# Row-stacked scores of the first attention: four heads at partitions 0 to 47 and four at 64 to 111

## The chip, the cores and the metric

The kernel runs on one core of a Trainium2 chip. A core has five engines that each run their own list of instructions in order: TensorE (PE, with PEld for its weight loads), VectorE (DVE), ScalarE (ACT), GpSimd (POOL) and SyncE (SP). In this kernel SP issues every DMA. Engines meet only at semaphores. The metric is the device time of one execution in microseconds (us); smaller is better.

## The reference

The program is two transformer layers on x of shape 16 x 128 x 256 with a context of the same shape. The first attention is the part that matters here:

```python
def _L0_xattn_ref(q, k, v):                 # B = 16, D = 128 channels, T = 256
    h = 8; d = D // h                       # 8 heads of 16 channels
    qn = _l2norm(q.reshape(B, h, d, Tq), axis=-2)
    kn = _l2norm(k.reshape(B, h, d, Tk), axis=-2)
    sm = softmax(5.0 * einsum('bhdq,bhdk->bhqk', qn, kn), axis=-1)
    return einsum('bhqk,bhdk->bhdq', sm, v.reshape(B, h, dv, Tk)).reshape(B, Dv, Tq)

x = x + _L0_xattn_ref(_layernorm(x), ctx, ctx)
x = x + _L0_ffn_ref(_layernorm(x), ...)     # quantised feed-forward
x = x + _L1_xattn_ref(_layernorm(x), ctx, ...)  # second attention, 16 query heads of 128
x = x + _L1_ffn_ref(_layernorm(x), ...)     # quantised gated feed-forward
```

## The kernel before

After a barrier that ends the preparation of the weights, four stages follow: the first attention (`part_a`), a feed-forward, the second attention and another feed-forward. Each engine's program is a Python generator that is advanced in steps. The first attention has 93 steps and the first feed-forward begins at step 93 (`B_START`), so on each engine every instruction of the first attention stands ahead of every instruction of the feed-forward.

In the first attention there are 16 batches of 4 units; a unit is two heads. Every piece of work has a lag in steps behind its batch or unit (`LOAD`, `STORE`, `GATHER`, `SCORE`, ...). Inside a step the order is that of the code. One batch goes like this:

- SP loads the rows of x and of the context (L226, L227). DVE and ACT normalise them; POOL squares them (L281); PE sums the squares of each head by a matmul with a block matrix (L405) and turns the context (L401); ACT and DVE make unit vectors (L322 to L324, L375); POOL splits these into a high and a low float16 half (L287, L289).
- SP stores both halves to DRAM (L254, two DMAs), and once they have landed reads them back as stacks (`GATHER`, L242 and L245): for each head the 16 channels lie on partitions 0 to 15 with other halves of the same on 16 to 31 and 32 to 47, high, low, high for q and high, high, low for k. One matmul over 48 partitions so gives the product in nearly float32 precision. The stacks hold all eight heads side by side and are double-buffered over batches. A gather waits until its store has landed (`stored`) and until the scores of the batch two earlier are done (`scores`). SP also turns the context halves by a DMA transpose (L231).
- PE makes the scores (L391): for a unit, two heads by two halves of 128 keys, four matmuls of 256 columns. The first unit of a batch waits for the whole stack (`stacked`). The two heads of a unit write to different PSUM banks.
- ACT exponentiates a unit in one instruction (L305). PE multiplies by the values and by ones for each pair of units (L422), at four column groups of 32; DVE divides (L336, L339), POOL adds the residual (L294).

The queue of SP is in order: per batch it holds the six gather DMAs of batch b, the two stores of batch b+1, the transpose of batch b+3 and the two loads of batch b+5, and then the next gather. The transfer sizes are 64 KB for a gather DMA and 128 KB for a store or load. On PE the order per batch is: scores of units 0 and 1, values of the batch before (units 2 and 3), scores of units 2 and 3, two transposes, the sum of squares of a later batch, values of units 0 and 1.

Of the kernel before, what the change touches and what calls it, by code (L numbers as in the profile page):

```python
# [18 lines left out]
F16 = mybir.dt.float16  # L19
# [6 lines left out]
P = 128  # L26
BATCHES = 16
D = 256
# [9 lines left out]
def wait(eng, sem, value):  # L38

    if value > 0:  # L40
        eng.wait_ge(sem, value)
# [104 lines left out]
def part_a(core, x_in, ctx_in):  # L146
# [3 lines left out]
    c, nc = core, core.nc  # L150
    HEADS, HD, PAIRS = 8, 16, 4
    STACK = 3 * HD
# [15 lines left out]

    halves = c.local("halves_a", [P, 2, 2, 2 * D], F16)
    ctx_hl = c.local("ctxhl_a", [P, 2, 2, D], F16)  # L170
    q_stack = c.local("q_stack", [STACK, 2, HEADS, D], F16)
    k_stack = c.local("k_stack", [STACK, 2, HEADS, D], F16)
    yc = c.local("yc_a", [P, 4, 2, D])
    stats = c.local("stats_a", [P, 2, 6])
    mv = c.local("mv_a", [P, 2, 2])
# [13 lines left out]
    stacked = [c.sem(f"a_stacked{n}") for n in range(2)]  # L189
# [5 lines left out]
    score_banks = lambda p: c.psum[:, 2 * p:2 * p + 2, :]  # L195
# [5 lines left out]
    def heads_of(v):  # L201


        m = v % PAIRS
        return (0, 4, 1, 5)[m], (2, 6, 3, 7)[m]

    def unit(s, lag):

        v = s - lag
        return v if 0 <= v < TOTAL else None  # L210

    def batch(s, lag):

        v = s - lag
        return v // PAIRS if 0 <= v < TOTAL and v % PAIRS == 0 else None

    def sync(eng):
        for s in range(STEPS):
            b = batch(s, LOAD)
            if b is not None:  # L220
                n = b % 4

                wait(eng, S["unit"], b - 3)
                wait(eng, S["vt"], b - 3)
                wait(eng, S["ctx_low"], b - 3)
                eng.dma_start(c.x_rows[:, b, :], x_in[b, :, :]).then_inc(loaded[n], 16)  # L226
                eng.dma_start(yc[:, n, 1, :], ctx_in[b, :, :]).then_inc(loaded[n], 16)  # L227
            b = batch(s, CTX_TURN)
            if b is not None:
                eng.wait_ge(S["ctx_low"], b + 1)  # L230
                eng.dma_start_transpose(c.ctx_t[:, b, :, :].rearrange("p s (k r) -> p (s k) r", k=2),  # L231
                                        ctx_hl[:, b % 2, :, :].rearrange("p s n -> p (s n)"))\
                   .then_inc(ctx_turned[b % 2], 16)
            b = batch(s, GATHER)
            if b is not None:
                p = b % 2

                eng.wait_ge(stored[p], 32 * (b // 2 + 1))
                wait(eng, S["scores"], PAIRS * (b - 1))
                src = split_dram[p].rearrange("s (h d) n -> s d h n", d=HD)  # L240
                for k, part in enumerate((0, 1, 0)):
                    eng.dma_start(q_stack[HD * k:HD * k + HD, p, :, :], src[part, :, :, 0:D])\  # L242
                       .then_inc(stacked[p], 16)
                for k, part in enumerate((0, 0, 1)):
                    eng.dma_start(k_stack[HD * k:HD * k + HD, p, :, :], src[part, :, :, D:2 * D])\  # L245
                       .then_inc(stacked[p], 16)
            b = batch(s, STORE)
            if b is not None:
                p = b % 2

                eng.wait_ge(S["low"], b + 1)
                wait(eng, stacked[p], 96 * (b // 2))
                for part in range(2):
                    eng.dma_start(split_dram[p, part], halves[:, p, part, :]).then_inc(stored[p], 16)  # L254
            yield
        for p in range(2):
            eng.wait_ge(ctx_turned[p], 16 * (BATCHES // 2))
# [121 lines left out]
    def tensor(eng):  # L379
        eng.wait_ge(c.consts_ready, 1)  # L380
        eng.wait_ge(S["ones"], 4)
        for s in range(STEPS):
            v = unit(s, SCORE)
            if v is not None:
                b, vp = v // PAIRS, v // PAIRS % 2
                if v % PAIRS == 0:
                    eng.wait_ge(stacked[vp], 96 * (b // 2 + 1))
                wait(eng, S["exps"], v - 1)
                for j, h in enumerate(heads_of(v)):
                    for k in range(2):  # L390
                        mm = eng.matmul(score_banks(v % 2)[:, j, D * k:D * k + D], k_stack[:, vp, h, P * k:P * k + P],  # L391
                                        q_stack[:, vp, h, :], start=True, stop=True)
                mm.then_inc(S["scores"], 1)
            b = batch(s, SUM)
            if b is not None:
                n = b % 4
                eng.wait_ge(loaded[n], 32 * (b // 4 + 1))

                wait(eng, S["v_evicted"], 2 * b)
                for k in range(2):  # L400
                    t = eng.transpose(vt_half(b)[:, P * k:P * k + P], yc[:, n, 1, P * k:P * k + P], c.ident[:, :])  # L401
                t.then_inc(S["vt"], 1)
                eng.wait_ge(S["sq"], b + 1)
                wait(eng, S["clipped"], b)
                eng.matmul(LEN_BANK, c.same_head[:, :], sq[:, b % 2, :], start=True, stop=True)\  # L405
                   .then_inc(S["lengths"], 1)
            v = unit(s, VALUES)
            if v is not None and v % 2:


                b, odd = v // PAIRS, v % PAIRS // 2
                to = value_bank(b % 2)
                if not odd:
                    eng.wait_ge(S["v_evicted"], 2 * (b + 1))
                    wait(eng, S["ratio"], b - 1)
                eng.wait_ge(S["exps"], v + 1)
                for k in range(2):
                    for what in range(2):
                        for g in range(4):
                            q, j = v % PAIRS - 1 + g // 2, g % 2  # L420
                            h = 2 * g + odd
                            mm = eng.matmul(to[2 * HD * g:2 * HD * (g + 1), D * what:D * what + D],  # L422
                                            ones[:, odd, :] if what else v_t[:, b % 4, k, h, :],
                                            probs[:, q, j, k, :], start=(odd == 0 and k == 0 and what == 0),
                                            stop=(odd == 1 and k == 1 and what == 1))
                mm.then_inc(S["values"], 1)
            yield

    return sync, pool, scalar, vector, tensor


# [454 lines left out]
HEADS, KV_HEADS, HEAD_DIM = 16, 4, 128  # L886
# [581 lines left out]
def program(nc, x, ctx_in, pos_ctx, pos_x, b_w1, b_w2, wq, wk, wv, wo, q_norm, k_norm, d_w1, d_w2, d_w3,  # L1468
            inv_freq, out):
    with ExitStack() as ctx:  # L1470
# [5 lines left out]
        barrier = end_part(core, 0)  # L1476
        core.new_part()
        first = part_a(core, x, ctx_in)

        core.new_part(FFN_B_AT)  # L1480
# [74 lines left out]
```

## Time and profile before

| | |
|---|---|
| three runs, us | 799.06, 797.79, 1745.51; median 799.06 |
| the profiled execution, us | 800.01 |
| its span (first to last instruction), us | 798.3 |
| mean granted TensorE clock | 0.961 |
| busy: PE, DVE, ACT, POOL | 85%, 83%, 78%, 67% |
| first attention: first gather DMA issued, first matmul of the feed-forward, us from the span's start | 86.39, 205.94 |

Busy times say which engine did how much; the idle times say what ended each wait. SPq rows are the DMA instructions as SP's queue issues them: their duration is that of the issue, not of the transfer, whose time to landing is listed apart. The timeline merges neighbouring instructions of one line into one row with their count.

### The profile page before, as it was taken

What the parts mean: (1) busy time and instruction counts of PE and PEld (TensorE: products, weight loads), DVE (VectorE), ACT (ScalarE), POOL (GpSimd) and SP (SyncE); (2) the same over time, 40 slices, a digit from 0 to 9 for tenths busy, and PEclk for the clock granted to TensorE, in tenths of its full rate; (3) what the DMA queues carried; (4) which work ended last, traced back from release to release, by engine and by line L of the source; (5) the groups of instructions that cost most, each with busy time, mean ns of one, the idle gap of its engine ahead of it and who ended that gap; (6) DMA issues with size and microseconds to landing.
All of it is one profiled execution on the core that took longest, in us unless ns stands there. A gap on an engine that the chain in (4) does not pass through costs nothing. (4 is left out here: it accounts for less than half of the span.)

```text
span 798.3 us, 17290 instructions
## 1 busy us (share of the span) xinstructions
PE 677.3 (85%) x5139; PEld 423.0 (53%) x5139; DVE 661.1 (83%) x1576; ACT 624.3 (78%) x2122; POOL 534.5 (67%) x764
## 2 busy tenths in 40 slices
PE   0075799999578678999999999999999999978995
PEld 0043255455234345666666666666666666645552
DVE  6756556764689769999999999999999999978994
ACT  0556477777399769999999999999999999968661
POOL 1413756663357888888788878887887888753673
PEclk9997599999799989999999999999999999999997
DMA  8502555542024356897887798788879787865244
GB/s 278 199 1 54 138 155 148 142 129 86 11 67 106 64 106 126 147 144 129 148 139 142 127 154 139 134 138 154 139 135 144 143 136 133 153 113 93 58 125 122
DMA packets 323795, 99.80 MB, mean 125 GB/s; under 512 B 294868, under 2 KB 322934, under 8 KB 323446
## 3 DMA queue, kind: packets, MB, share of 16 engines
q1 hardware_dynamic: 323702, 98.70, 61.7%
q8 instruction: 41, 0.67, 0.4%
q14 instruction: 52, 0.43, 0.2%
HBM read 20.01 MB, written 6.29 MB: 33 GB/s over the span
## 5 line engine op out<-in xcount | busy, mean ns | idle before, releaser
L1235 ACT ACTIVATE psum<-psum,arena 128x256 f32<-128x256 f32 x256 | 135.9, 531 | 21.1 <-DVE arena L1355 21.0
L1311 DVE SCALAR_TENSOR_TENSOR arena<-psum,arena 128x256 f16<-128x256 f32 x256 | 110.9, 474 | 1.1 <-ACT arena L1252 1.1
L1252 ACT ACTIVATE arena<-psum,arena 128x256 f16<-128x256 f32 x256 | 100.3, 474 | 7.4 <-issue 3.4
L1444 PE MATMUL psum<-arena 128*128 128x512 f16 x384 | 94.2, 381 | 8.1 <-DVE arena L1338 7.9
L1189 POOL TENSOR_TENSOR arena<-arena 128x512 f32<-128x512 f32 x64 | 81.1, 1267 | 27.8 <-DVE arena L1330 27.8
L1406 PE MATMUL psum<-wq_t,arena 128*128 128x512 f16 x384 | 94.5, 383 | 5.5 <-ACT arena L1266 2.8
L1431 PE MATMUL psum<-arena 128*128 128x256 f16 x768 | 95.6, 275 | 1.0 <-DMA arena<-arena 0.8
L1459 PE MATMUL psum<-wo_t,arena 128*128 128x256 f16 x768 | 95.0, 274 | 0.1
L305 ACT ACTIVATE arena<-psum 128x1024 f32<-128x1024 f32 x64 | 63.1, 1019 | 33.2 <-PE psum L391 33.2
L1459 PEld LDWEIGHTS psum<-wo_t,arena 128*128 128x128 f16 x768 | 75.5, 98 | 23.2 <-issue 1.1
L1220 POOL TENSOR_TENSOR arena<-arena 128x512 f16<-128x512 f32 x64 | 74.1, 1157 | 20.0 <-DVE arena L1355 19.9
L1431 PEld LDWEIGHTS psum<-arena 128*128 128x128 f16 x768 | 75.3, 99 | 11.4 <-DMA arena<-arena 1.6
L1351 DVE TENSOR_REDUCE arena<-psum 128x4 f32<-128x1024 f32 x64 | 77.8, 1215 | 2.7 <-PE psum L1431 2.4
L1330 DVE TENSOR_TENSOR arena<-psum,arena 128x1024 f32<-128x1024 f32 x64 | 78.4, 1225 | 1.1 <-PE psum L1406 1.1
L1266 ACT ACTIVATE arena<-psum 128x128 f32<-128x128 f32 x256 | 68.2, 304 | 10.6 <-DVE arena L1330 10.6
L1417 PE MATMUL psum<-wkv_t,ctx_t 128*128 128x256 f16 x384 | 54.3, 279 | 13.2 <-DVE arena L1370 12.6
L1366 DVE SCALAR_TENSOR_TENSOR arena<-psum,arena 128x256 f32<-128x256 f32 x128 | 56.1, 480 | 9.3 <-ACT arena L1301 6.7
L1223 POOL TENSOR_TENSOR arena<-arena 128x256 f32<-128x256 f32 x64 | 46.3, 724 | 23.7 <-DVE arena L1366 23.6
L422 PE MATMUL psum<-arena 128*32 128x256 f32 x1024 | 61.9, 383 | 0.0
L1266 ACT ACTIVATION_READ_ACCUMULATOR arena<-psum 128x1 f32 x256 | 60.8, 238 | 0.0
L1444 PEld LDWEIGHTS psum<-arena 128*128 128x128 f16 x384 | 33.7, 97 | 48.0 <-issue 13.6
L1417 PEld LDWEIGHTS psum<-wkv_t,ctx_t 128*128 128x128 f16 x384 | 33.2, 99 | 46.9 <-DVE arena L1370 42.3
(187 smaller groups left out, 1612.5 us busy)
## 6 DMA issues: line engine op xcount, KB each, us to landing
arena<-split_scratch SPq DMA_DIRECT2D x96, 64.0 KB, 2.6
arena<-arena SPq DMA_TRANSPOSE x272, 3.3
split_scratch<-arena SPq DMA_DIRECT2D x32, 128.0 KB, 2.1
arena<-in_L_ffn_w SPq DMA_DIRECT2D x2, 1024.0 KB, 6.8
x_rows<-in_L_xattn_Wq SPq DMA_DIRECT2D x1, 2048.0 KB, 14.4
ctx_t<-in_L_xattn_Wo SPq DMA_DIRECT2D x1, 2048.0 KB, 12.4
x_rows<-in_x SPq DMA_DIRECT2D x16, 128.0 KB, 2.3
arena<-in_ctx SPq DMA_DIRECT2D x16, 128.0 KB, 2.5
```

Of the source, the lines that this page charges most:

```text
L1189: eng.tensor_tensor(straight(q_rot[:, :, :]), straight(q_cs[:, 0, :, :]), swapped(q_cs[:, 1, :, :]), ALU.add).then_inc(S["q_rot"], 1)
L1235: last = eng.activation(s_banks(u)[:, h, :], s_banks(u)[:, h, :], ACT.Exp, bias=bias[:, u % 2, h:h + 1], scale=r_q(u)[:, h:h + 1], accum_o ...
L1252: hi = eng.activation(p_hl[:, u % 2, 0, h, :], s_banks(u)[:, h, :], ACT.Copy, scale=share[:, u % 2, h:h + 1])
L1266: last = eng.activation(junk[:, h, :], Q_BANK[:, P * h:P * h + P], ACT.Square, accum_out=sums[:, u % 2, h:h + 1])
L1311: last = eng.scalar_tensor_tensor(p_hl[:, u % 2, 1, h, :], s_banks(u)[:, h, :], share[:, u % 2, h:h + 1], p_hl[:, u % 2, 0, h, :], ALU.mul ...
L1330: eng.tensor_tensor(q_cs[:, :, :, :], Q_BANK.rearrange("p (h d) -> p h d", h=SHARE).unsqueeze(1).broadcast_to([P, 2, SHARE, HEAD_DIM]), tu ...
L1351: eng.tensor_reduce(top[:, u % 2, :], s_banks(u), AX.X, ALU.max).then_inc(S["top"], 1)
L1406: mm = eng.matmul(Q_BANK, y_t[:, b % 2, x, k, :], c.wq_t[:, w, k, SHARE * P * g:SHARE * P * g + SHARE * P], start=(n == 0), stop=(n == 5))
L1417: mm = eng.matmul(KV_BANK[:, KEYS * row:KEYS * row + KEYS], x_t, c.wkv_t[:, w, k, g, :, :].rearrange("p a d -> p (a d)"), start=(n == 0), ...
L1431: mm = eng.matmul(s_banks(u)[:, h, :], q_head(u, q, h), k_keys(u, k), start=(n == 0), stop=(n == 2))
L1444: mm = eng.matmul(A_BANK, v[:, u % V_SLOTS, x, k, :], p_t[:, u % 2, w, :, k, :], start=(n == 0), stop=(n == 5))
L1459: mm = eng.matmul(O_BANK, a_t[:, u % 2, a, P * h:P * h + P], c.wo_t[:, w, SHARE * g + h, :], start=(g == 0 and h == 0 and n == 0), stop=(g ...
```

## The change

The stacks have 112 partitions in place of 48 and four heads side by side in place of eight: heads 0 to 3 on partitions 0 to 47, heads 4 to 7 on 64 to 111. A unit takes one head of each group, and its four matmuls alternate between the groups (and with them between the two PSUM banks). Each gather DMA is split in two, one for each group, of 32 KB in place of 64; the semaphore's targets double. In the values' loop only the index changes by which a head finds its unit's probabilities.

```diff
-    q_stack = c.local("q_stack", [STACK, 2, HEADS, D], F16)
-    k_stack = c.local("k_stack", [STACK, 2, HEADS, D], F16)
+    q_stack = c.local("q_stack", [64 + STACK, 2, HEADS // 2, D], F16)
+    k_stack = c.local("k_stack", [64 + STACK, 2, HEADS // 2, D], F16)
...
-        return (0, 4, 1, 5)[m], (2, 6, 3, 7)[m]
+        return (0, 2, 1, 3)[m], (4, 6, 5, 7)[m]
...
                 for k, part in enumerate((0, 1, 0)):
-                    eng.dma_start(q_stack[HD * k:HD * k + HD, p, :, :], src[part, :, :, 0:D])\
-                       .then_inc(stacked[p], 16)
+                    for j in range(2):
+                        eng.dma_start(q_stack[64 * j + HD * k:64 * j + HD * k + HD, p, :, :],
+                                      src[part, :, 4 * j:4 * j + 4, 0:D]).then_inc(stacked[p], 16)
                 for k, part in enumerate((0, 0, 1)):
-                    eng.dma_start(k_stack[HD * k:HD * k + HD, p, :, :], src[part, :, :, D:2 * D])\
-                       .then_inc(stacked[p], 16)
+                    for j in range(2):
+                        eng.dma_start(k_stack[64 * j + HD * k:64 * j + HD * k + HD, p, :, :],
+                                      src[part, :, 4 * j:4 * j + 4, D:2 * D]).then_inc(stacked[p], 16)
...
-                wait(eng, stacked[p], 96 * (b // 2))
+                wait(eng, stacked[p], 192 * (b // 2))
...
-                    eng.wait_ge(stacked[vp], 96 * (b // 2 + 1))
+                    eng.wait_ge(stacked[vp], 192 * (b // 2 + 1))
                 wait(eng, S["exps"], v - 1)
-                for j, h in enumerate(heads_of(v)):
-                    for k in range(2):
-                        mm = eng.matmul(score_banks(v % 2)[:, j, D * k:D * k + D], k_stack[:, vp, h, P * k:P * k + P],
-                                        q_stack[:, vp, h, :], start=True, stop=True)
+                for k in range(2):
+                    for j, h in enumerate(heads_of(v)):
+                        half = slice(64 * j, 64 * j + STACK)
+                        mm = eng.matmul(score_banks(v % 2)[:, j, D * k:D * k + D],
+                                        k_stack[half, vp, h % 4, P * k:P * k + P],
+                                        q_stack[half, vp, h % 4, :], start=True, stop=True)
...
-                            q, j = v % PAIRS - 1 + g // 2, g % 2
+                            q, j = v % PAIRS - 1 + g % 2, g // 2
```

SP's queue before, from one gather to the next; the names in brackets are the semaphores that an instruction waits for:

```order
L242 DMA arena<-split_scratch 16x8x256 [waits a_scores,a_stored0]
L242 DMA arena<-split_scratch 16x8x256 x2
L245 DMA arena<-split_scratch 16x8x256 x3
L254 DMA split_scratch<-arena 128x512 [waits a_stacked1,a_low]
L254 DMA split_scratch<-arena 128x512
L231 DMA_TRANSPOSE ctx_t<-arena 128x4x128 [waits a_ctx_low]
L226 DMA x_rows<-in_x 128x256 [waits a_ctx_low,a_vt,a_unit]
L227 DMA arena<-in_ctx 128x256
```

The same place in SP's queue of the changed kernel:

```order
L243 DMA arena<-split_scratch 16x4x256 [waits a_scores,a_stored0]
L243 DMA arena<-split_scratch 16x4x256 x5
L247 DMA arena<-split_scratch 16x4x256 x6
L256 DMA split_scratch<-arena 128x512 [waits a_stacked1,a_low]
L256 DMA split_scratch<-arena 128x512
L231 DMA_TRANSPOSE ctx_t<-arena 128x4x128 [waits a_ctx_low]
L226 DMA x_rows<-in_x 128x256 [waits a_ctx_low,a_vt,a_unit]
L227 DMA arena<-in_ctx 128x256
```

Nothing changes place; twelve DMAs of half the rows (16x4x256) stand where six (16x8x256) stood, ahead of the store of the next batch.

PE's list in the changed kernel, from the first unit of a batch to the values of its units 0 and 1 (L394 scores, L426 values, L405 transposes, L409 sum of squares):

```order
L394 MATMUL psum<-arena 128x256 [waits a_exps,a_stacked0]
L394 MATMUL psum<-arena 128x256 x3
L394 MATMUL psum<-arena 128x256 [waits a_exps]
L394 MATMUL psum<-arena 128x256 x3
L426 MATMUL psum<-arena 32x256 [waits a_exps]
L426 MATMUL psum<-arena 32x256 x15
L394 MATMUL psum<-arena 128x256 [waits a_exps]
L394 MATMUL psum<-arena 128x256 x3
L394 MATMUL psum<-arena 128x256 [waits a_exps]
L394 MATMUL psum<-arena 128x256 x3
L405 MATMUL psum<-ident,arena 128x128 [waits a_v_evicted,a_loaded2]
```

The number and order of PE's rows are those of before; only the operands' partitions and the order of the four matmuls inside a unit differ. Behind the row that waits for the stack stands all the rest of PE's work.

## Rows read from the trace of the kernel before

**Rows 1.** Timeline of PE in one batch: start us, us, what, count.
```profile
144.37 1.04 PE L391 MATMUL psum<-arena 48*128 48x256 f16 x8
145.34 1.93 PE L422 MATMUL psum<-arena 128*32 128x256 f32 x32
147.21 1.04 PE L391 MATMUL psum<-arena 48*128 48x256 f16 x8
148.19 0.44 PE L401 MATMUL psum<-ident,arena 128*128 128x128 f32 x2
148.46 1.02 PE L405 MATMUL psum<-arena,same_head 128*128 128x512 f32 x2
149.41 1.93 PE L422 MATMUL psum<-arena 128*32 128x256 f32 x32
```

**Rows 2.** Waits of PEld, 91 to 206 us: waited for, us, times, longest.
```profile
PEld psum L391 <- DMA arena<-split_scratch: 1.5, 1, 1.5
```

**Rows 3.** Timeline of SP's queue over one batch in which it never waits.
```profile
99.76 1.32 SPq L242 DMA_DIRECT2D arena<-split_scratch  x3
101.12 1.38 SPq L245 DMA_DIRECT2D arena<-split_scratch  x3
102.60 0.85 SPq L254 DMA_DIRECT2D split_scratch<-arena  x2
103.49 1.19 SPq L231 DMA_TRANSPOSE ctx_t<-arena  x1
104.79 0.52 SPq L226 DMA_DIRECT2D x_rows<-in_x  x1
105.35 0.43 SPq L227 DMA_DIRECT2D arena<-in_ctx  x1
105.90 2.48 SPq L242 DMA_DIRECT2D arena<-split_scratch  x3
```

**Rows 4.** SP's queue: first gather of the stage, one long transpose, last gather.
```profile
86.39 1.38 SPq L242 DMA_DIRECT2D arena<-split_scratch  x3
...
90.18 2.26 SPq L231 DMA_TRANSPOSE ctx_t<-arena  x1
...
191.53 2.46 SPq L242 DMA_DIRECT2D arena<-split_scratch  x3
194.03 1.38 SPq L245 DMA_DIRECT2D arena<-split_scratch  x3
```

**Rows 5.** Waits of SP's queue, 91 to 206 us.
```profile
SPq L231 <- POOL arena L273: 5.0, 7, 0.9
SPq L254 <- POOL arena L289: 3.6, 5, 1.1
SPq L41 <- PE psum L391: 1.7, 2, 0.9
SPq L242 <- DMA split_scratch<-arena: 0.9, 2, 0.5
```

**Rows 6.** Issues at the start: 8 KB in 16 rows, and 2048 KB.
```profile
0.78 0.41 SPq L937 DMA_DIRECT2D arena<-in_pos_BxS  x1
...
9.21 0.47 SPq L945 DMA_DIRECT2D x_rows<-in_L_xattn_Wq  x1
```

**Rows 7.** Source views: issue durations in ns, min/median/max.
```profile
L940 SPq DMA_DIRECT2D arena<-in_L_xattn_k_norm_w x1: 223/223/223, 2.1 to 2.1; - x1
```
**Rows 8.** The gather line, the same view.
```profile
L242 SPq DMA_DIRECT2D arena<-split_scratch x48: 318/431/1702, 86.4 to 193.6; - x48
```

**Rows 9.** DMA issues of the page: count, KB each, median us to landing.
```profile
arena<-split_scratch SPq DMA_DIRECT2D x96, 64.0 KB, 2.6
...
split_scratch<-arena SPq DMA_DIRECT2D x32, 128.0 KB, 2.1
```

**Rows 10.** PE at the end of the stage: batch 15's scores, values, first feed-forward matmul.
```profile
198.54 1.04 PE L391 MATMUL psum<-arena 48*128 48x256 f16 x8
199.51 1.93 PE L422 MATMUL psum<-arena 128*32 128x256 f32 x32
201.38 1.04 PE L391 MATMUL psum<-arena 48*128 48x256 f16 x8
202.35 3.66 PE L422 MATMUL psum<-arena 128*32 128x256 f32 x64
205.94 0.39 PE L860 MATMUL psum<-cs_b,minus_off 128*128 128x512 f16 x1
```

**Rows 11.** Stretches: us, busy of PE, PEld, DVE, ACT, POOL (counts), PEclk, DMA share, GB/s.
```profile
100.00:104.00 4.00, 4.00 (x51) 2.49 (x50) 1.12 (x3) 2.60 (x3) 1.67 (x2) 1.00 0.64 190
...
208.00:212.00 4.00, 0.00 (x0) 0.00 (x0) 2.97 (x14) 0.00 (x0) 1.92 (x6) 0.86 0.00 0
```

## The prediction, on record before the changed kernel ran

> **What bounds the kernel now.** I went from the stage table of the page (the first attention runs from about 86 to 206 us) to the timeline of PE, then to PE's waits, and then to the queue of SP, since the change touches both. In the timeline of PE a batch is a closed row of work: 144.37 to 151.28 us, a period of 6.9 us in which scores (0.97 us from their start to the next start), values (1.87), transposes (0.27) and the sum of squares (0.95) follow each other [rows 1]. For the stacks PE waited once, 1.5 us, in the whole stage [rows 2]. So PE sets the pace, and shorter scores look like a gain. The second thing to see is how close SP is behind. From 99.76 to 105.90 SP never waits, and one batch takes it 6.14 us of pure issuing [rows 3]. Over the stage, from the first gather at 86.39 to the end of the last at 195.41 [rows 4], that is 109.0 us, and its waits add up to 5.0 + 3.6 + 1.7 + 0.9 = 11.2 us [rows 5]. SP is a second engine at its limit: 97.8 of 109.0 us are issuing.
>
> **What the change does, part by part.**
>
> *PE's scores.* Eight matmuls of two units take 0.97 us, 0.12 each [rows 1]. If matmuls in different row groups overlap in pairs, half goes: 0.49 us for each pair of units, 0.97 per batch. The trace has no row-grouped matmul. The nearest row is the values: 32 passes in four column groups of a length of 1.93 us, 0.06 each, against about 0.5 for one pass of twice the columns in the sum of squares (two passes in 1.02 us) [rows 1], so groups of columns do overlap. Bounds: nothing and 0.97 us per batch. I take the whole, since the two heads also write different banks; in the forecast it counts only in the last batch, 0.9 us.
>
> The Trainium skill ("TensorE: Matmul & The Clock Gate", part 3, packing small matmuls) says that matmuls on distinct row groups run concurrently, and that 32-row tiles gained about three times. By that rule PE's period would be 5.9 us and 16 batches would give back up to 15.5 us, were PE still the bound; no run here shows it yet.
>
> *SP's queue.* Six gather DMAs become twelve. From the first gather's issue to the store behind it the six take 102.60 − 99.76 = 2.84 us, 0.473 each with the gap [rows 3]. What does one of half the size cost? The issue hardly depends on size: 8 KB in 16 rows took 0.41 us, 2048 KB took 0.47 [rows 6], a gather of 64 KB 0.43, a store or load of 128 KB 0.42 to 0.52 [rows 3, 8]. The cheapest gather took 0.318 [rows 8] and a single row of 0.5 KB 0.223 [rows 7]; these are the lower bounds (with 0.04 us of gap, 0.36 and 0.26). Half a gather still has 16 rows of partitions, so I take 0.473: twelve take 5.68 us, and SP's batch becomes 6.14 + 2.84 = 8.98 us. That is above PE's 6.9 (or 5.9), so SP becomes the bound and PE waits for the stacks.
>
> The sum along SP's queue, from the first gather at 86.39 [rows 4]:
> - Batches 0 to 10, each with store, transpose and loads of later batches behind the gathers: 11 × 8.98 = 98.8.
> - Batches 11 to 14: the loads are over and from 13 on the transposes too, and the next gather must wait for its store to land. The second store is issued 0.45 after the first and lands 2.1 later [rows 3, 9]: 4 × (5.68 + 0.45 + 2.1) = 32.9.
> - The last gather: eleven issues, then 2.6 us until the twelfth has landed [rows 9]: 5.2 + 2.6 = 7.8.
> - Stalls. One transpose took 2.26 us in place of 1.19, one gather of three 2.48 in place of 1.32 [rows 3, 4]. Their total is what is left: regular issuing is 11 × 6.14 + 2 × 5.03 + 2 × 3.73 + 2.8 = 87.9 us (without loads 5.03, without transpose too 3.73), with 11.2 of waits 99.1; 9.9 us of the 109.0 remain, on 161 issues. With 257 issues that makes 15.8 if each issue has its share, 12.6 if they come with time. I take 14.
>
> The twelfth gather DMA of batch 15 so lands at 86.4 + 98.8 + 32.9 + 7.8 + 14 = 239.9 us. Before, the scores of batch 15 started at 198.54 and the feed-forward's first matmul at 205.94 [rows 10]; of these 7.4 us the faster scores take 0.9, so the stage ends at 246.4 instead of 205.94. On each engine the feed-forward stands behind the stage, so nothing hides the 40.5 us, and nothing later gets shorter. The profiled execution took 800.0 (span 798.3), which is 0.9 above the median of 799.06: 840.5 by the profile, **839** against the median.
>
> *Waits behind the gathers.* The store, transpose and loads now stand 2.84 us later behind each gather; their consumers are whole batches away. The nearest is the load of batch b+5, which waits for unit vectors of batch b+2 made behind the values on PE; PE now stands idle about 4 us per batch, so they are ready. The wait for the scores of two batches earlier (1.7 us in all [rows 5]) ends early for the same reason. The doubled semaphore targets and the new index cost nothing. The same bytes move: 768 rows of 512 bytes for a batch, in twelve DMAs.
>
> **The rivals.**
>
> 1. *The issue follows the size* (the other side: not slower). SP stays hidden as long as twelve issues plus their stalls fit into the 11.2 us of waits, 0.7 us per batch: an issue of at most 0.26 us, or 0.22 with the stalls. For it: 0.223 for a single row [rows 7]. Against it: 16 rows at 0.41 and 2048 KB at 0.47 [rows 6]. At 0.215 the queue gains 0.22 × 16 + 96 × 0.062 = 9.5 us, less than its waits, and the stage ends 1.7 + 0.9 us earlier: **797**. Even were the six more DMAs free, SP's own 97.8 us bound the gain at 11.2 + 0.9: 788. That is why faster by over 2% has next to no chance. The Trainium skill ("DMA: Bandwidth & Descriptors", issuing engines are not separate DMA queues) calls the sequencer's time to initiate a DMA usually small relative to the DMA itself; by that rule splitting costs about nothing, and the time would be this rival's. Here the issue takes 0.43 us of 2.6 to landing, but there are eleven such DMAs in a batch of 6.9 us.
> 2. *A price in between*: 0.318 + 0.04 for each [rows 8]. Twelve take 4.3, 1.4 us less than I sum for each of 16 batches: 839 − 22 = **817**. Against it: it is the minimum of 48, and the median is 0.431.
> 3. *The clock falls.* PE's work is 5.9 us of a period of about 9.9 with stalls, so it stands idle 4.0 us at a stretch. After the last matmul of the stage (ending near 206.3) the stretch from 208 to 212 has a mean of 0.86: full speed until about 210.9, 4.6 us later, then 1.2 GHz [rows 10, 11]. That is close. At half speed PE's batch would be nearly 12 us, above SP's 9.9, so it would then run without a pause; a few batches would lose about 2 us each and the last 6 us once: **850**.
> 4. *The pairs don't overlap*: PE's batch stays 6.9, still under SP's, and only the last 0.9 us are lost: 840. It is not told from the forecast by the time.
>
> **How the numbers follow.** The forecast (with rival 4) has 0.80. Its own range goes from 830 (0.41 + 0.04 per issue: −4.5; stalls as before, 10: −4) to 848 (stalls of 16, a slower landing, some of rival 3). Rival 3 has 0.07, rival 2 0.05, rival 1 0.07, something faster still 0.01. A range of 820 to 852 leaves out rivals 1 and most of 2 and the end of 3, and some of the unknown in the stalls. Two per cent of 799 is 16 us, about what a measurement of this kernel can tell from none: slower than 815 are the forecast, rival 3 and more than half of rival 2, 0.90; within 2% 0.09; faster 0.01.
>
> **What would show it.** In the changed kernel's profile: SP's gather lines with 96 issues each at a median near 0.43 us; an interval between gathers of 9 to 10 us in place of 6.1 to 7.9, with almost no waits of SP's queue before batch 11; PE waiting for DMA about 4 us once per batch at the scores; scores of two units in about 0.6 us in place of 1.04; the first matmul of the feed-forward near 246 us; and everything after it as long as before. I am wrong if the issues come out at 0.3 us or less, or if the next gather waits for something else than the queue, such as unit vectors or the landing of the stores.

## The result and the profile after

The changed kernel takes 833.6 us (median of four runs, 831.62 to 835.03) against 798.67: a ratio of 1.044 with a 95% interval of 1.041 to 1.047, so slower by 4.4%. One of the four runs of the kernel before took 1745.51 us; it is left out of the ratio. The forecast was 839, its range 820 to 852. The profiled execution took 834.02 with a span of 832.3; before it was 800.01 and 798.3.

The timeline of SP's queue over one batch of the changed kernel; it answers to [rows 3]:

```profile
96.43 2.78 SPq L243 DMA_DIRECT2D arena<-split_scratch  x6
99.25 2.77 SPq L247 DMA_DIRECT2D arena<-split_scratch  x6
102.11 0.84 SPq L256 DMA_DIRECT2D split_scratch<-arena  x2
103.00 1.19 SPq L231 DMA_TRANSPOSE ctx_t<-arena  x1
104.30 0.51 SPq L226 DMA_DIRECT2D x_rows<-in_x  x1
104.86 0.43 SPq L227 DMA_DIRECT2D arena<-in_ctx  x1
105.39 2.72 SPq L243 DMA_DIRECT2D arena<-split_scratch  x6
```

From gather to gather it is 8.96 us (8.98 were forecast), and there is no wait in it. The source view of one gather line, in ns, min/median/max, answers to [rows 8]; the DMA issues of the page answer to [rows 9]:

```profile
L247 SPq DMA_DIRECT2D arena<-split_scratch x96: 313/426/1847, 88.9 to 233.4; - x96
```
```profile
arena<-split_scratch SPq DMA_DIRECT2D x192, 32.0 KB, 1.8
...
split_scratch<-arena SPq DMA_DIRECT2D x32, 128.0 KB, 1.8
```

Half the bytes cost the same 0.43 us to issue. What did get shorter is the landing, 1.8 us in place of 2.6. The waits of SP's queue in the stage, 86 to 245 us, answer to [rows 5]:

```profile
SPq L243 <- DMA split_scratch<-arena: 2.7, 2, 1.4
SPq L231 <- POOL arena L275: 1.9, 3, 0.8
```

11.2 us of waits before, 4.6 now, and only 1.9 of these for another engine: SP is the bound. PE's weight loads, which stand ahead of its matmuls, wait instead, where [rows 2] had one wait of 1.5 us:

```profile
PEld psum L394 <- DMA arena<-split_scratch: 45.0, 16, 4.9
```

PE in one batch and at the end of the stage, which answers to [rows 1, 10]; the brackets give the idle time of PE and what ended it:

```profile
142.80 0.61 PE L394 MATMUL psum<-arena 48*128 48x256 f16 x8 [1.54 <-DMA arena<-split_scratch]
143.34 1.93 PE L426 MATMUL psum<-arena 128*32 128x256 f32 x32
...
161.70 1.03 PE L394 MATMUL psum<-arena 48*128 48x256 f16 x8 [3.75 <-DMA arena<-split_scratch]
162.66 3.64 PE L426 MATMUL psum<-arena 128*32 128x256 f32 x32
...
235.23 0.61 PE L394 MATMUL psum<-arena 48*128 48x256 f16 x8 [2.94 <-DMA arena<-split_scratch]
235.77 3.19 PE L426 MATMUL psum<-arena 128*32 128x256 f32 x32
238.90 0.98 PE L394 MATMUL psum<-arena 48*128 48x256 f16 x8
239.81 3.66 PE L426 MATMUL psum<-arena 128*32 128x256 f32 x64
243.40 0.39 PE L864 MATMUL psum<-cs_b,minus_off 128*128 128x512 f16 x1
```

Three things are to be seen. The pairing works: eight score matmuls take 0.61 us where they took 1.04, and the next work starts 0.54 after them where it was 0.97, so 0.43 us of 0.97 are gone for two units. (The four matmuls of a unit also alternate between the PSUM banks now; no run does that without row groups, so the 0.43 us belong to the two together.) The stage ends at 243.40, 37.5 us later than before. And after some of the pauses the clock is at its lower level: scores of 1.03, values of 3.64.

```profile
140.00:160.00 20.00, 13.72 (x192) 6.48 (x184) 11.89 (x27) 12.14 (x19) 10.87 (x14) 1.00 0.39 108
160.00:180.00 20.00, 15.46 (x168) 7.01 (x168) 10.07 (x20) 10.75 (x16) 9.16 (x13) 0.83 0.40 110
```

These two stretches (the columns of [rows 11]) show how a granted clock of 0.83 raises PE's busy time from 13.7 to 15.5 us for fewer instructions. PE's busy share is no measure of work here.

### The profile page after: what moved, and what is told of

Its sections match the earlier page's. It is cut to its first block and busy times, and to the rows that moved or that the text cites. A ratio compares the mean times of both kernels' runs of the same rounds, so it can differ in the third digit from the quotient of the medians.

```text
span 832.3 us, 17386 instructions
## 1 busy us (share of the span) xinstructions
PE 679.5 (82%) x5139; PEld 415.2 (50%) x5139; DVE 662.2 (80%) x1576; ACT 625.5 (75%) x2122; POOL 534.2 (64%) x764
## 5 line engine op out<-in xcount | busy, mean ns | idle before, releaser
L426 PE MATMUL psum<-arena 128*32 128x256 f32 x1024 | 74.8, 442 | 0.0
L289 POOL CAST arena<-arena 128x512 f16<-128x512 f32 x16 | 10.8, 673 | 71.2 <-DVE arena L377 71.2
```

## The experiments

Theory A is the forecast's: SP's queue bounds the stage, and what counts is how many DMAs it issues. Its rival B puts the loss on the new layout, the alternation or the falling clock.

**split_only**: only the DMAs, without row groups.

```diff
-                    eng.dma_start(q_stack[HD * k:HD * k + HD, p, :, :], src[part, :, :, 0:D])\
-                       .then_inc(stacked[p], 16)
+                    for j in range(2):
+                        eng.dma_start(q_stack[HD * k:HD * k + HD, p, 4 * j:4 * j + 4, :],
+                                      src[part, :, 4 * j:4 * j + 4, 0:D]).then_inc(stacked[p], 16)
...
```

> The kernel before, with each gather DMA split in two by heads (12 of 32 KB for a batch) into the old stacks of 48 partitions; PE's scores stay as they were. Theory A (SP's queue is the bound, its cost is the number of issues): the stage is as long as in the changed kernel but for the faster scores of the last batch, 0.9 us: 834 to 836 us. Theory B (the slowdown comes from the new layout, the alternation on PE or the clock that falls behind it): about 799 us, as before.

Measured: 834.5 us, ratio 1.0455 (1.0426 to 1.0484). The split alone makes the whole loss, on the old layout and with the old order on PE; B falls.

**tiny_rows and tiny_one**: the kernel before with six more DMAs for a batch, of 16 rows and of one row.

```diff
+                for n in range(6):
+                    eng.dma_start(spare[0:16, p, n, :], split_dram[p, 0, 0:16, 0:8]).then_inc(stacked[p], 16)
...
```

In tiny_one `spare[0:1, ...]` and `split_dram[p, 0, 0:1, 0:8]` stand in their places.

> The kernel before with six more DMAs for a batch behind the gathers, each of 16 rows of 16 bytes (256 bytes) into a spare tile. Theory A (number of issues): as the kernel with twelve halved gathers, 832 to 838 us. Rival (issue follows rows or bytes): 799 to 806 us.

> The same with each of the six extra DMAs a single row of 16 bytes. If an issue costs the same whatever its rows: 832 to 838 us. If a single row costs the 0.22 us that the constants' loads showed: 6 x 0.26 = 1.6 us for a batch, 25 us and 6 of stalls less 11 of waits that are free: 815 to 820 us.

Measured: 833.15 us, 1.0405 (1.038 to 1.043), and 814.89, 1.0184 (1.0156 to 1.0211), just under the 815 to 820 of a cheap single row. The source view of the added line, first with 16 rows, then with one:

```profile
L249 SPq DMA_DIRECT2D arena<-split_scratch x96: 323/421/1890, 88.9 to 233.7; - x96
```
```profile
L249 SPq DMA_DIRECT2D arena<-split_scratch x96: 228/253/326, 88.8 to 216.0; - x96
```

256 bytes in 16 rows cost 0.42 us of the queue, as do 32, 64 and 128 KB; the time is that of the changed kernel. A single row costs 0.25, and the kernel loses less than half as much. So neither the bytes nor the number of transfers (six more in both runs) are the price but the issue. Of the sizes that were run only the single row issues faster; between one row and 16 nothing was tried.

**split_one**: one of the six gather DMAs split, seven for a batch.

```diff
+                    for a, z in (((0, 4), (4, 8)) if n < 1 else ((0, 8),)):
+                        eng.dma_start(stack[HD * k:HD * k + HD, p, a:z, :], src[part, :, a:z, at:at + D])\
+                           .then_inc(stacked[p], 16)
...
```

> The kernel before with one of the six gather DMAs split (seven for a batch). Theory A with SP's free 11.2 us: 16 x 0.47 = 7.6 us and 1 of stalls are less than that: 798 to 801 us. Rival (each further issue costs its share of the whole, 35 us / 6): 804 to 806 us.

Measured: 799.04 us, 0.9997 (0.9984 to 1.0011). The first further DMA is free: the loss has a threshold. SP's waits in the stage, 11.2 us before, are down to 5.2 (2.1 + 1.4 + 1.0 + 0.7 in the same view); they paid for it.

**half_act**: the changed kernel, the upper group's six gather DMAs issued by ACT, ahead of the exponential in its program.

```diff
+            b = batch(s, GATHER)
+            if b is not None:
+                p, j = b % 2, 1
+                eng.wait_ge(stored[p], 32 * (b // 2 + 1))
+                wait(eng, S["scores"], PAIRS * (b - 1))
...
```

> The changed kernel, with the six gather DMAs of the upper group issued by ACT in place of SP. Theory A: SP issues six again (6.1 us for a batch and stalls), but ACT pays 6 x 0.47 = 2.8 us on top of 5.7 us of its own work, 8.5 us for a batch, so ACT becomes the bound: 815 to 822 us. If issuing were free on ACT: 786 to 798 us. If not SP's queue but the twelve transfers themselves were the bound: 833 us.

Measured: 812.69 us in two runs, 1.0167 (1.0129 to 1.0205), 2 us below the 815 to 822 that were expected. ACT's timeline in one batch, and PE's wait for ACT from 86 to 230 us:

```profile
144.43 0.20 ACT L330 ACTIVATE arena<-arena 128x1 f32<-128x1 f32 x1
144.49 1.30 ACTq L310 DMA_DIRECT2D arena<-split_scratch  x3
145.81 3.24 ACTq L313 DMA_DIRECT2D arena<-split_scratch  x3
149.15 2.86 ACT L319 ACTIVATE arena<-psum 128x1024 f32<-128x1024 f32 x3 [4.52 <-issue]
```
```profile
PE psum L406 <- ACT arena L319: 23.3, 22, 3.5
```

ACT computes nothing while it issues, 4.5 us here, and PE then waits for the exponentials; for the stacks it waited once, 1.1 us. Another queue helps, but its engine pays about the same for a DMA (a median of 0.45 us), stalls among them.

**filler**: the changed kernel with more work on PE.

```diff
+                for again in range(2):
+                    eng.matmul(LEN_BANK, c.same_head[:, :], sq[:, b % 2, :], start=True, stop=True)
```

> The changed kernel, with the sum of squares of each batch computed three times over into the same bank (only the last signals), 1.9 us more of work on PE for a batch in the time in which it waits for the stacks. Theory A: PE's 7.9 us stay under SP's 9.2 to 9.4, the clock stays at 2.4 GHz and the time at 831 to 835 us. If the falling clock had a part in the slowdown: 820 to 828 us. If PE's work were on the path: 16 x 1.9 = 30 us more, over 860.

Measured: 838.28 us, 1.0465 (1.0438 to 1.0492): 4.7 us above the changed kernel and 3 above what was expected. The waits of SP's queue show it:

```profile
SPq L256 <- POOL arena L291: 8.7, 4, 6.9
```

The longer sum of squares comes ahead of the unit vectors, and a store now waited 6.9 us for them. It is the first store, before the stage gets going, and the first gather behind it issues at 89.53 where the changed kernel has 86.11:

```profile
89.53 2.77 SPq L243 DMA_DIRECT2D arena<-split_scratch  x6
```

That is 3.4 of the 4.7 us; the stretch behind the stage has 1.9 more (590.8 against 588.9). From the first gather to the feed-forward's first matmul (246.15) this kernel takes 156.6 us, the changed one 157.3. So 1.9 us more of work for each batch cost nothing inside the stage, where 30 would be due: PE is off the path. On the clock it is no clean test, since the edit added waits; but from 100 to 240 us the granted clock rose in six of seven stretches of 20 us, to 1.00 in five of them, and the stage became hardly shorter. The changed kernel's own waits set a limit: the first scores of all 16 batches waited for the stacks, and SP waited for another engine 1.9 us. By these rows the falling clock can't have cost more than that ahead of the last batch, where it cost 1.7.

**merged_only and merged_pairs**: the issues taken away, without and with the row groups. DRAM now holds for each channel its three stack rows (high, low, high beside high, high, low), so that 48 rows are one DMA. The gather and the store of merged_pairs, against the changed kernel:

```diff
+                src = split_dram[p].rearrange("(h d) (t a) n -> (d t) h (a n)", d=HD, a=2)
+                for j in range(2):
+                    eng.dma_start(stack[64 * j:64 * j + STACK, p, :, :], src[:, 4 * j:4 * j + 4, :]).then_inc(stacked[p], 16)
...
-                for part in range(2):
-                    eng.dma_start(split_dram[p, part], halves[:, p, part, :]).then_inc(stored[p], 16)
+                four = halves[:, p, :, :].rearrange("p s (a n) -> p (s a) n", a=2)
+                for to, at in ((slice(0, 2), slice(0, 2)), (slice(2, 4), slice(2, 0, -1)), (slice(4, 6), slice(0, 4, 3))):
+                    eng.dma_start(split_dram[p, :, to, :], four[:, at, :]).then_inc(stored[p], 16)
```

> The kernel before, with the stack laid out in DRAM by three stores of 128 KB (row order channel by channel, high, low, high beside high, high, low) and gathered by one DMA of 384 KB for a batch; PE as before. Theory A: SP needs 4.2 us for a batch, PE's 6.9 us bound the stage as before: 796 to 800 us. Theory B says the same, so this run is the base for the next one.

> The changed kernel's row groups and alternating scores, with three stores and two gather DMAs of 192 KB for a batch in place of two and twelve. Theory A: SP needs 4.7 us for a batch and no longer bounds; the scores of two units take 0.54 in place of 0.97 us, 16 x 0.86 = 13.8 us less on PE: 784 to 789 us, if ACT's 5.7 us for a batch leave PE its 6.0. Theory B: no faster than 799 us.

Measured: 798.16 us, 0.9989 (0.998 to 0.9997), and 795.0 us, 0.9945 (0.9927 to 0.9963). Relieving SP is worth next to nothing by itself, as expected. With it the row groups no longer cost, but of 13.8 us expected 4.5 came, 3.2 of them against merged_only. PE's timeline of merged_pairs, one batch and the next:

```profile
150.95 0.61 PE L388 MATMUL psum<-arena 48*128 48x256 f16 x8
151.49 1.93 PE L420 MATMUL psum<-arena 128*32 128x256 f32 x32
153.36 0.61 PE L388 MATMUL psum<-arena 48*128 48x256 f16 x8
154.19 0.41 PE L399 MATMUL psum<-ident,arena 128*128 128x128 f32 x2 [0.22 <-DVE arena L352]
156.07 1.12 PE L403 MATMUL psum<-arena,same_head 128*128 128x512 f32 x2 [1.47 <-POOL arena L277]
157.13 1.93 PE L420 MATMUL psum<-arena 128*32 128x256 f32 x32
158.99 0.61 PE L388 MATMUL psum<-arena 48*128 48x256 f16 x8
```

This batch takes 8.04 us and the one ahead of it (from 144.65) 6.3: on every second one PE waits 1.5 us for POOL's squares (L277). The kernel before has the same pattern, only hidden from my reading. Its next batch after that of [rows 1] has this row:

```profile
156.29 1.13 PE L405 MATMUL psum<-arena,same_head 128*128 128x512 f32 x2 [0.76 <-POOL arena L281]
```

Its scores start at 144.37, 151.28 and 159.21: 6.9 and 7.9 by turns, 7.4 on average. POOL's list in merged_pairs explains it:

```profile
151.28 0.73 POOL L283 CAST arena<-arena 128x512 f16<-128x512 f32 x1 [3.30 <-DVE arena L371]
152.08 1.16 POOL L285 TENSOR_TENSOR arena<-arena 128x512 f16<-128x512 f32 x1
153.21 0.72 POOL L290 TENSOR_TENSOR x_rows<-arena,x_rows 128x256 f32<-128x256 f32 x1
153.87 0.40 POOL L267 CAST arena<-arena 128x256 f16<-128x256 f32 x1
154.35 0.67 POOL L269 TENSOR_TENSOR arena<-arena 128x256 f16<-128x256 f32 x1
154.98 1.04 POOL L277 TENSOR_TENSOR arena<-arena 128x512 f32<-128x512 f32 x1
```

The squares stand behind the halves of the unit vectors (L283, L285), the residual (L290) and the context's halves (L267, L269), and all of these hang on DVE's work behind the values of the batch before. Shorter scores only lengthen PE's wait in this loop.

Two of the five waits for the squares cost more than themselves. The values behind them took 3.59 and 3.40 us in place of 1.93, and these batches 9.7:

```profile
126.77 3.59 PE L420 MATMUL psum<-arena 128*32 128x256 f32 x32
```

From 126.77 to 130.30 the granted clock was 0.52, after PE had waited 1.48 us; behind the other three such waits the values took 1.93 us. So 3.3 us of what the pairs failed to bring went to the clock.

**only_pool and pairs_pool**: POOL squares first, then adds the residual, then makes the context's halves.

```diff
-    LOAD, STATS, RSTD, ROWS, CTX_HALVES, CTX_TURN, SQUARE, SUM, CLIP, CTX, LENGTH = 0, 3, 4, 5, 5, 7, 6, 8, 9, 10, 11
+    LOAD, STATS, RSTD, ROWS, CTX_HALVES, CTX_TURN, SQUARE, SUM, CLIP, CTX, LENGTH = 0, 3, 4, 5, 5, 7, 5, 8, 9, 10, 11
...
+            b = batch(s, SQUARE)
...
+            b = batch(s - 1, RESIDUAL)
...
```

Both blocks now stand ahead of CTX_HALVES; the squares come a step earlier, and the residual a step later.

> The kernel with two gather DMAs and paired scores (795 us), whose batches took 6.3 and 8.0 us by turns: on every second one PE waited about 1.5 us for POOL's squares, which stand behind the residual and the context's halves. Here POOL squares first, then adds the residual, then makes the context's halves. Theory C (this chain over DVE and POOL held the pairs' gain back): no wait for the squares, every batch at 6.0 to 6.4 us, 16 x 1.1 = 17 us less than before: 780 to 787 us. Rival (ACT's exponentials are the next bound, or the clock falls in PE's pauses): 790 to 795 us.

> The same order on POOL in the kernel with one gather DMA and unpaired scores (798 us), whose batches took 6.9 and 7.9 us by turns. Theory C: every batch at PE's own 6.9 us, half a microsecond less on twelve batches: 791 to 794 us. Rival: 797 to 799 us.

Measured: 786.69 us, 0.9836 (0.9821 to 0.985), and 797.27, 0.9975 (0.9965 to 0.9985). PE's timeline of pairs_pool:

```profile
121.47 0.61 PE L388 MATMUL psum<-arena 48*128 48x256 f16 x8
122.01 1.93 PE L420 MATMUL psum<-arena 128*32 128x256 f32 x32
123.88 0.61 PE L388 MATMUL psum<-arena 48*128 48x256 f16 x8
124.70 0.41 PE L399 MATMUL psum<-ident,arena 128*128 128x128 f32 x2 [0.21 <-DVE arena L352]
124.95 1.02 PE L403 MATMUL psum<-arena,same_head 128*128 128x512 f32 x2
125.90 1.93 PE L420 MATMUL psum<-arena 128*32 128x256 f32 x32
```

The next batch starts at 127.77: 6.30 us, with no wait for the squares. From the second to the twelfth every batch takes 6.3 us (one 6.6), and none has values at the lower clock. Theory C holds, and this is the fastest version here, 1.6% ahead of the kernel before. Its stage ends at 195.49, against 205.94 before. only_pool misses what was expected by 3 us and lands in the rival's range, 797 to 799, although each of its batches takes 6.9 us (scores at 103.16, 110.07, 116.98), as Theory C says. The head of the stage took the gain back: with the context's halves behind the squares SP's first transpose came later, and behind it in SP's queue the first gather:

```profile
87.07 1.21 SPq L230 DMA_TRANSPOSE ctx_t<-arena  x1
88.42 0.49 SPq L225 DMA_DIRECT2D x_rows<-in_x  x1
88.94 0.43 SPq L226 DMA_DIRECT2D arena<-in_ctx  x1
89.42 0.43 SPq L240 DMA_DIRECT2D arena<-split_scratch  x1
```

In merged_only the first transpose issued at 74.09 (here at 76.89), that gather at 86.90, and the first scores started at 91.61, here at 94.19. The 2.6 us come off the gain; pairs_pool pays 3.0 (94.12 against 91.07 in merged_pairs). So only_pool's stage ends at 204.16, 2.2 us before merged_only's.

## Why the prediction was right, and where it was off

- *The bound moves to SP.* Shown from both sides: twelve gathers without row groups are as slow (834.5), row groups without the twelve gathers are not slow (795.0).
- *The issue doesn't follow the size.* Right: 0.426 us at 32 KB, 0.421 at 256 bytes. Rival 1's price holds for a single row alone (0.253). The issue is small beside one transfer (0.43 us of 1.8 to landing), but 17 DMAs add up to 8.96 us for a batch, and that is the bound. The Trainium skill ("DMA: Bandwidth & Descriptors", issuing engines are not separate DMA queues) calls the sequencer's time to initiate a DMA usually small relative to the DMA itself. For one DMA the trace agrees; as a guide to this kernel's time it fails.
- *The sum along the queue.* Gather to gather 8.96 for 8.98. The last gather landed near 235.2 in place of 239.9. The 4.7 us between are: stalls 12.1 in place of 14 (what is left of 147.7 us of queue after the regular issues and the 2.7 us of waits for the store; at the three transposes to which the view puts the other 1.9 us of waits the timeline has no gap; the stalls come nearer with time than with issues), 1.3 because the store landed in 1.8 us and, as long as a transpose stood behind it, the next gather hardly waited for it at all, 0.9 in the last gather, mostly its landing of 1.8, and 0.6 of start and rounding.
- *PE's pause.* "About 4 us once per batch" was 2.8 (45.0 us in 16 waits). PE's batch took 6.5 us at full clock (142.80 to 149.32) in place of 5.9, and more where the clock fell. SP gave the pace, so the time did not feel it.
- *The last batch.* From its scores to the feed-forward 8.2 us in place of 6.5: at the lower clock the values took 3.19 and not 1.93. Rival 3 came true in kind, in 160 to 180 with a clock of 0.83, but not in size, since SP gave the pace anyway. Its reading that a pause of 4.0 us is "close" to a fall was too mild: here the clock fell around pauses of 2.3 to 2.9 us too.
- *After the stage.* I let nothing get shorter; the rest took 588.9 us against 592.4. In the profiles of the ten experiments the same stretch takes 589.6 to 592.5, with kernels that are identical there, so most of these 3.5 us is scatter; no run shows a cause. Stage 3.0 (4.7 less, 1.7 more in the last batch) and rest 3.5 us make the 6.5 by which 834.0 stays under the forecast of 840.5 for the profile. That the forecast came within 1% is in part luck: its errors were of both signs. Its sum also gives 839.6, not 839.
- *PE sets the pace.* This reading of the kernel before was too simple, though it cost the forecast nothing. One batch of 6.9 us was taken for all; the next one takes 7.9. The limit of gain in rival 1 (788) would therefore have been out of reach too: with SP relieved and the pairs in place the kernel stood at 795. Only the new order on POOL brought 786.7.
- *Row groups overlap.* The upper bound was 0.49 us for two units, the rows give 0.43. The Trainium skill ("TensorE: Matmul & The Clock Gate", part 3, packing small matmuls) has matmuls of distinct row groups run concurrently. The trace agrees for two groups of 48 rows: 1.8 times as fast from start to next start (0.97 to 0.54 us), with the banks alternating as well.

## What to carry to other kernels

Count DMA instructions per queue and period as you would count engine time: here each costs its queue about 0.47 us with the gap, whether it moves 256 bytes in 16 rows or 128 KB, and a queue that waits for 0.7 us per batch takes one more and not six. If a layout for PE needs more pieces, lay the data out in DRAM so that a single DMA brings them. And before a faster engine is credited with its saving, read two or three periods in a row: an engine that waits in every second one is in a loop with others, and the loop has to be shortened first.

## What the runs showed of the hardware

- The queue stalls 1.0 to 1.4 us now and then, whatever stands next (a gather, a load, a transpose [rows 4]): about 10 us of 109 before and 12 of 148 after, so nearly with time and not with the number of DMAs (161 and 257).
- TensorE's clock was at 1.2 GHz (granted 0.50) in the values that began at 162.66, after scores that waited 3.75 us, and at 2.4 GHz (granted 1.00) in those that began at 143.34, after a wait of 1.54 us. At 235.23, after 2.94 us, the scores still ran at full clock, and it fell in the values behind them (3.19 us, granted 0.58). In merged_pairs it fell after 1.48 us in one batch and not after the same wait in another, so the length of the last pause alone doesn't tell.
- A DMA from ACT's queue keeps ACT from computing as long as it issues: a median of 0.45 us each, and 4.5 us for six with a stall.
